# First attention of a gated cross-attention kernel: score products of two steps issued in alternating row halves, and the exponential of odd steps taken straight from PSUM with a bias

## The reference, cut to what matters

```python
xn = _layernorm(x, ln_gamma, ln_beta)
q = (xn @ w_q).reshape(B, SQ, 16, 64)
k, v = split(context @ w_kv)                      # (B, 120, 16, 64) each
scores = einsum('bqhd,bkhd->bhqk', q * 64**-0.5, k)
attn = softmax(scores, axis=-1)
out = einsum('bhqk,bkhd->bqhd', attn, v).reshape(B, SQ, 1024)
out = out @ w_out + b_out
return out * tanh(gate)
```

## Time and profile before

| What | us |
|---|---|
| median of three runs | 334.52 |
| the three runs | 334.09, 334.52, 336.31 |
| span of the profiled execution | 334.5 |
| PE busy | 317.7 (95%) |
| DVE busy | 195.4 (58%) |
| ACT busy | 161.1 (48%) |
| POOL busy | 71.7 (21%) |

### The profile page before, as it was taken

One profiled execution on the slowest core, in us unless ns is written; L12 is line 12 of the kernel. 1 busy time (PEld: TensorE's weight loads), 2 busy tenths in 40 slices (PEclk: granted clock), 3 DMA queues, 4 the chain that ended last, 5 costly groups with the idle time before them and its releaser, 6 DMA issues.

```text
span 334.5 us, 6100 instructions
## 1 busy us (share of the span) xinstructions
PE 317.7 (95%) x2241; PEld 273.2 (82%) x2241; DVE 195.4 (58%) x586; ACT 161.1 (48%) x278; POOL 71.7 (21%) x92
## 2 busy tenths in 40 slices
PE   1999999999999998899996999999999999999995
PEld 1578877888888887798984997889999888998994
DVE  3779768977998986246868483942434162112112
ACT  2483447765664445323353647627533553534530
POOL 1174015667734332010045410100010000000000
PEclk9999999999999999899999999999999999999999
DMA  7799000000000000430000000000000001000001
GB/s 211 233 307 185 0 0 2 3 4 11 19 0 2 0 2 3 145 139 1 0 2 1 2 0 2 0 0 2 3 1 2 0 0 33 0 2 2 0 0 34
DMA packets 10013, 11.31 MB, mean 34 GB/s; under 512 B 1049, under 2 KB 6833, under 8 KB 9984
## 3 DMA queue, kind: packets, MB, share of 16 engines
q1 hardware_dynamic: 9600, 10.55, 10.4%
q0 software_dynamic: 384, 0.36, 1.0%
HBM read 10.39 MB, written 0.52 MB: 33 GB/s over the span
## 4 chain that ended last, share of the span: by engine, by line
PE 82%; DVE 11%; issue 2%; POOL 2%; DMA 2%; ACT 0%; SPq 0%; DVEq 0%
PE bank L1024 28%; PE bank L875 9%; PE bank L876 9%; PE bank L877 8%; PE bank L822 8%; PE bank L831 4%; PE bank L860 4%; DVE xhat_sb L654 3%; PE bank L846 3%; DMA ctx_tok_sb<-in_ctx 2%; PE bank L910 2%; DVE sum_sb L593 2%; DVE negmax_sb L585 1%; PE bank L943 1%; PE bank L957 1%
## 5 line engine op out<-in xcount | busy, mean ns | idle before, releaser
L557 ACT ACTIVATE hT_sb<-bank,cols_sb 128x512 f32<-128x512 f32 x104 | 69.9, 687 | 82.7 <-PE bank L877 81.9
L799 DVE SCALAR_TENSOR_TENSOR x_sb<-bank,wts_sb,x_sb 128x128 f32<-128x128 f32 x128 | 36.0, 344 | 84.2 <-PE bank L1024 84.2
L1024 PEld LDWEIGHTS bank<-we_sb,hT_sb 128*128 128x128 f32 x576 | 66.5, 192 | 1.1
L1024 PE MATMUL bank<-we_sb,hT_sb 128*128 128x128 f32 x576 | 67.2, 275 | 0.0
L462 POOL TENSOR_TENSOR p_sb<-p_sb,recip_sb 128x480 f32<-128x480 f32 x32 | 31.6, 986 | 58.1 <-DVE recip_sb L596 58.1
L822 PE MATMUL bank<-kT_sb,qT_sb 64*128 64x120 f32 x256 | 36.8, 284 | 0.0
L822 PEld LDWEIGHTS bank<-kT_sb,qT_sb 64*128 64x128 f32 x256 | 30.8, 187 | 5.8 <-issue 5.2
L1024 PEld LDWEIGHTS bank<-w_sb,hT_sb 128*128 128x128 f32 x256 | 31.8, 198 | 1.6 <-issue 0.9
L1024 PE MATMUL bank<-w_sb,hT_sb 128*128 128x128 f32 x256 | 32.5, 282 | 0.0
L875 PE MATMUL bank<-xnT_lo_sb,we_hi_sb 128*128 128x512 f32 x72 | 30.4, 422 | 0.0
L876 PE MATMUL bank<-xnT_hi_sb,we_hi_sb 128*128 128x512 f32 x72 | 28.5, 396 | 0.0
(11 more groups left out here) (159 smaller groups left out, 476.0 us busy)
## 6 DMA issues: line engine op xcount, KB each, us to landing
we_sb<-in_L_ffn_We SPq DMA_DIRECT2D x1, 2048.0 KB, 8.3
w_kv_sb<-in_L_xattn_w_kv SPq DMA_DIRECT2D x2, 512.0 KB, 6.6
...
```

Source lines behind the costliest of these rows:

```text
L557: nc.scalar.activation(hT[:, u % 2, c, :], ps(item)[:, :], ACT.Relu if n == 1 else ACT.Silu, bias=cols[:, col:col + 1]).then_inc(read(item ...
L799: last = nc.vector.scalar_tensor_tensor(out=x[:, b, :], in0=ps(item)[:, C * i:C * (i + 1)], scalar=w, in1=x[:, b, :], op0=ALU.mult, op1=AL ...
L1024: last = nc.tensor.matmul(dst[:, C * i:C * (i + 1)], hT[:, slot, c, 128 * i:128 * (i + 1)], wb[:, e, c, :], start=(c == 0), stop=(c == chu ...
```

## The change

1. On TensorE S(i) and S(i+1) are issued together at the even item i, into two banks, and product by product the lower row half (step i) and the upper (step i+1) alternate. At odd items there is no S.
2. S uses four banks (0, 1, 5, 7) in place of two; O is left with bank 4 alone, and other fills with bank 6, which Y has too (`q0` with 4 and 6).
3. The late queries stand as four and four chunks behind items 0 and 1, where they were three, two and three behind items 0, 1 and 2.
4. In odd steps DVE no longer subtracts. It scales the maximum by -1/8 (a `tensor_scalar` on 128x4, L600 of the new kernel), and ACT takes four exponentials of 128x120, one for each head, from PSUM with that number as the bias (L532 of the new kernel). They stand where the one exponential stood, behind the copies of T and O.

```diff
--- before.py
+++ after.py
@@ -91,7 +91,7 @@
 
     schedule += [("q0", c, 0) for c in range(CH)]
 
-    late_queries = ((0, 1, 2), (3, 4), (5, 6, 7))
+    late_queries = ((0, 1, 2, 3), (4, 5, 6, 7))
     for i, chunks in enumerate(late_queries):
         schedule.append(("attend", i))
         schedule += [("q0", c, 1) for c in chunks]
@@ -152,11 +152,12 @@
 
     FILLS = ("ctxT", "cols", "v0", "k0", "xT", "q0", "logits", "wT", "b2", "k1", "v1", "q1", "s1", "pT1", "o1",
              "r1", "up")
+    S0_BANKS = (0, 1, 5, 7)
     turn = 0
     step = -1
     for item in schedule:
         if item[0] in FILLS and 0 <= step < STEPS + LY - 1:
-            spare = (4, 5, 7) if item[0] == "q0" else (0, 1) if item[0] == "up" else (7,)
+            spare = (4, 6) if item[0] == "q0" else (0, 1) if item[0] == "up" else (6,)
             plan(item, spare[turn % len(spare)])
             turn += 1
         elif item[0] in FILLS:
@@ -166,12 +167,13 @@
             plan(item, 6 + unit_at[item[1:]] % 2)
         elif item[0] == "attend":
             i = step = item[1]
-            if i < STEPS:
-                plan(("s0", i), i % 2)
+            if i < STEPS and i % 2 == 0:
+                plan(("s0", i), S0_BANKS[i % 4])
+                plan(("s0", i + 1), S0_BANKS[i % 4 + 1])
             if 0 <= i - LT < STEPS:
                 plan(("pT0", i - LT), 2 + i % 2)
             if 0 <= i - LPV < STEPS and (i - LPV) % 2:
-                plan(("o0", i - LPV), 4 + (i - LPV) // 2 % 2)
+                plan(("o0", i - LPV), 4)
             if 0 <= i - LY < STEPS and (i - LY) % GROUPS == GROUPS - 1:
                 plan(("y0", (i - LY) // GROUPS), 6)
 
@@ -326,6 +328,7 @@
         ident_ready = sem("ident_ready")
         consts_ready = sem("consts_ready")
         exps0_ready = sem("exps0_ready")
+        bias0_ready = sem("bias0_ready")
         recip_ready = sem("recip_ready")
         tanh_ready = sem("tanh_ready")
         dve_chain = sem("dve_chain")
@@ -517,10 +520,18 @@
                             wait_full(act, ("y0", b - 2))
                         copy_out(("o0", j), oT[:, b % 2, half * CH // 2:(half + 1) * CH // 2, :],
                                  ps(("o0", j))[:, :].rearrange("p (c q) -> p c q", q=128))
-                    if i < STEPS:
+                    if i < STEPS and i % 2 == 0:
                         wait_read(act, ("s0", i))
                         nc.scalar.activation(p0[i % 4], p0[i % 4], ACT.Exp, scale=SCALE0) \
                             .then_inc(exps0_ready, 1)
+                    elif i < STEPS:
+                        act.wait_ge(bias0_ready, i // 2 + 1)
+                        if i >= 4:
+                            wait_full(act, ("pT0", i - 4))
+                        for h in range(HG):
+                            last = nc.scalar.activation(p0[i % 4][:, h, :], ps(("s0", i))[:, SK * h:SK * (h + 1)],
+                                                        ACT.Exp, bias=negmax[:, 1, h:h + 1], scale=SCALE0)
+                        last.then_inc(read(("s0", i)), 1)
                 elif kind == "logits":
                     bs = half_of(item[2])
                     shifted += 1
@@ -582,14 +593,23 @@
                     key = ("s0", i)
                     s = ps(key)[:, 0:HG * SK].rearrange("p (h k) -> p h k", h=HG)
                     wait_full(dve, key)
+                    if i % 2 and i >= 2:
+                        wait_read(dve, ("s0", i - 2))
                     link(nc.vector.tensor_reduce(negmax[:, i % 2, :], s, AX, ALU.max))
-                    if i >= 4:
-                        wait_full(dve, ("pT0", i - 4))
-                    nc.vector.tensor_tensor(p0[i % 4], s, negmax[:, i % 2, :].unsqueeze(2)
-                                            .broadcast_to([128, HG, SK]), ALU.subtract).then_inc(read(key), 1)
+                    if i % 2:
+                        nc.vector.tensor_scalar(negmax[:, 1, :], negmax[:, 1, :], -SCALE0, None, ALU.mult) \
+                            .then_inc(bias0_ready, 1)
+                    else:
+                        if i >= 4:
+                            wait_full(dve, ("pT0", i - 4))
+                        nc.vector.tensor_tensor(p0[i % 4], s, negmax[:, 0, :].unsqueeze(2)
+                                                .broadcast_to([128, HG, SK]), ALU.subtract).then_inc(read(key), 1)
                 j = i - 1
                 if 0 <= j < STEPS:
-                    dve.wait_ge(exps0_ready, j + 1)
+                    if j % 2:
+                        wait_read(dve, ("s0", j))
+                    else:
+                        dve.wait_ge(exps0_ready, j // 2 + 1)
                     link(nc.vector.tensor_reduce(sum0[:, j % 2, :], p0[j % 4], AX, ALU.add))
                     if j >= 2:
                         dve.wait_ge(probs_ready, j - 1)
@@ -809,19 +829,21 @@
         def _(pe):
             def attend(i):
 
-                if i < STEPS:
-                    key = ("s0", i)
+                if i < STEPS and i % 2 == 0:
                     b, g = i // GROUPS, i % GROUPS
-                    dst = open_bank(pe, key)
-                    r0 = DH * (g % 2)
+                    dst = [open_bank(pe, ("s0", i)), open_bank(pe, ("s0", i + 1))]
                     for j in range(HG):
                         c = (g // 2) * HG + j
                         if b % HB == 0:
                             wait_read(pe, ("q0", c, b // HB))
                             wait_read(pe, ("k0", c, b // HB))
-                        last = nc.tensor.matmul(dst[:, SK * j:SK * (j + 1)], qT[r0:r0 + DH, c, 128 * b:128 * (b + 1)],
-                                                kT[r0:r0 + DH, c, SK * b:SK * (b + 1)], start=True, stop=True)
-                    last.then_inc(full(key), 1)
+                        for odd in range(2):
+                            r0 = DH * odd
+                            last = nc.tensor.matmul(dst[odd][:, SK * j:SK * (j + 1)],
+                                                    qT[r0:r0 + DH, c, 128 * b:128 * (b + 1)],
+                                                    kT[r0:r0 + DH, c, SK * b:SK * (b + 1)], start=True, stop=True)
+                            if j == HG - 1:
+                                last.then_inc(full(("s0", i + odd)), 1)
                 m = i - LT
                 if 0 <= m < STEPS:
                     key = ("pT0", m)
```

## The result

The changed kernel took 333.18 us (median of 20 runs, 331.92 to 334.91); the kernel before, in 20 runs beside it, 334.58. The ratio is 0.995, with a 95% interval of 0.993 to 0.997: faster by 1.4 us where 5.0 were forecast. It lies in the range of 326 to 335, but by the bound of 1% it is "no change", to which the prediction gave 0.35. The rest of this document is about the 3.6 us that are missing.

A forecast was written before the change was run, and what follows sets the result against it. PE was taken to pace from S(0) to S(18), then DVE to about 129 us; 0.7 + 2.3 + 2.0 + 0.5 - 0.4 = 5.1 off 334.5 gave 329.4, stated as 329.5, range 327.5 to 331.8 (8 in 10: 326 to 335).

The forecast's parts named there:

- Scores on PE: Score matmuls on PE: alternating row halves overlap fully, so two steps' scores take 1.08 us instead of 2.16.
- rival 1: Score matmuls on PE: row halves don't overlap, 1.96 us a pair, total 333.5 to 335, say 334.3; chance 0.2.
- The second T of a pair: Transposes on PE: one group directly behind another needs no array shape change, so 0.45 us in place of 0.58.
- The start: First attention steps: late queries and exponentials delay S(2) to about 50 us; at S(12) the lead is only 0.7 us.
- rival 3: PE's clock falls because of holes, including 1.7 and 1.4 us at T(1) and T(2): total 337.5; chance 0.07.
- The scaling on DVE: Odd steps on DVE: POOL holds up the 128x4 scaling, 0.4 us to the next start, between 0.1 and 0.57 + 0.1.
- a period: Four attention steps where PE paces: 8.05 us of PE work plus a 0.5 wait, 8.6 against 10.48 before.
- the pair without Y: Two attention steps without a Y product, added to one four-step period between S(12) and S(18): 3.6 us.
- DVE's stretch: Step 18 to about 129 us: DVE paces; waits of 1.2 us go and six odd steps give 0.17 each, 2.0 to 2.2.
- rival 2: Odd steps on DVE: scaling not held up, bank stalls smaller, odd steps 1.55 us, total 326.5; chance 0.15.
- The tail: Behind the attention: transposed router weights share bank 6 with the first expert product and wait for its updates, losing 0.4 us.
- ACT: Odd steps on ACT: four exponentials take at most 1.6 us, hidden except where a copy of T is waited for.

The follow-up runs named there:

- the run with halves in turn: Changed kernel with all score products of the lower row half issued first, then all of the upper, without alternation: 336.03 us, ratio 1.001.
- the fillings: Changed kernel with matmuls that compute nothing of the result put in PE's idle holes, two ahead of T(1) and one ahead of T(2): 333.39 us, ratio 0.994.
- the kernel without the scaling: Changed kernel with queries scaled by -1/8 when copied from PSUM and the minimum used directly as the exponentials' bias: 330.27 us, ratio 0.983.
- SP's run: Changed kernel with the eight small loads that POOL issued between its multiplications issued by SP instead: 334.3 us, ratio 0.994.

## Why the prediction was right and wrong

**Scores on PE: right.** 1.08 for two steps was forecast from O, and 1.08 was measured; rival 1 is out, and the run with halves in turn shows that the order of the products does it. The second T of a pair was put at 0.45 and took 0.53 behind Y and 0.55 behind a wait (75.36 to 75.91).

**The start: right but for the clock.** S(2) at 50.19 (forecast about 50), T(1) at 54.70 (54.4), T(2) at 56.56 (56.3). Then O(1) and S(6) ran at the lower clock: S(6) at 58.95 against 57.8, S(12) at 72.61 against 70.7.

**The clock: the step that failed first.** The fall was in the text only as rival 3, with a whole period at the lower level and 337.5 as its time, at 0.07; the sum had no term for it, though the text itself had reckoned with holes of 1.7 and 1.4 us at T(1) and T(2). It came at the two holes that the rival named (T(1) and T(2)), but for some 3 us only. Its size is read from kernels that differ in the fillings alone: the maximum of step 31 at 121.51 without and 119.92 with them, 1.6 us, and this in the execution compared, not in a rare one. The second part is the tail. Of the kernel before, 10 of 23, 14 of 27 and 13 of 18 executions in three sets on one chip ran at the full clock; of the changed kernel none of 20 did, and 19 lost more than one fall's 0.005. (For the 20 executions of before that were timed beside those, the clocks aren't on record; 13 of them took 334.8 us or less, the longest time that went with a full clock elsewhere.) In the span from T(31) to the end both profiled executions have one fall and so the same length (204.2 and 204.25), which hides this in the pair of traces; in the medians of the times it doesn't cancel. The trace of before had shown one dip, in an execution 2 us above the usual one, and the prediction took that as the standing state: it subtracted its 5.1 from the span of an execution with a dip and compared the result with times, where the usual execution of before has none.

The Trainium skill, TensorE: Matmul & The Clock Gate, says under HAM oscillation that idle gaps between bursts bring the clock down. Rows of the changed kernel agree (0.72 behind holes of 1.69 and 1.24), and the fitted fillings remove it there (1.00 in 55 to 60 us). But the kernel before kept 1.00 from 175 to 185 us, around a hole of 2.86 ahead of 179.59, where the changed kernel fell to 0.67 behind the same hole, and the kernel without the scaling kept it behind 1.70 and 0.71; so the gaps allow a fall rather than force it.

**The scaling on DVE: the term that was mis-sized.** The term was 0.4 with 0.57 + 0.1 as the upper bound. Measured were 0.50 behind a multiplication alone (to the next start 0.42), 0.17 with POOL idle, and 1.04 and 1.11 where POOL multiplies, issues a transfer and subtracts. The bound had counted a second operation of POOL's but not the transfer between them, which is part of what POOL does in steps 8 to 15, and which SP's run shows to be half of the cost. So the waits at T at 75.36 and 84.66 were 1.00 and 1.07 instead of 0.5, and a period 9.24 instead of 8.6. (A wait of 1.16 at 66.12 and one of 1.19 at 94.08 stand behind scalings of 0.50 and 0.17: the transfer doesn't explain those.) From S(12) to S(18) that is 0.64 for the period and 0.78 for the pair without Y (4.38 in place of 3.6), 1.4 us together: what is left of the deficit of 3.0 at step 18 when the clock's 1.6 is taken off. That the two add up so exactly is in part chance: at S(12) another 0.3 was missing beside the clock, and the 0.3 by which DVE was to start later behind S(18) didn't come (1.19 against 1.12 before).

**DVE's stretch: right in sum, by two errors that cancel.** From step 18 to step 31 the lead was to grow by 2.0; it grew by 2.35. The forecast held up each scaling by POOL, 0.4 to the next start. Of the seven scalings there five took 0.17 and weren't held (0.07 to the next start at 100.88), which is what rival 2 said, and gave some 0.3 each more than the forecast; and one new wait of 1.22 took most of that back. That one wasn't forecast: the logits' product now fills bank 6, which Y has just used, so PE can start it only when DVE has updated x, and DVE stands until it is done:

```profile
119.42 0.32 DVE L622 SCALAR_TENSOR_TENSOR x_sb<-bank,gA_sb,x_sb 128x128 f32<-128x128 f32 x1
119.79 1.06 PE L965 MATMUL bank<-gate_w_sb,xnT_sb 128*128 128x8 f32 x8 [0.53 <-DVE x_sb L622]
120.96 0.19 DVE L716 TENSOR_TENSOR logits_sb<-bank,gate_b_row_sb 128x32 f32<-128x32 f32 x1 [1.22 <-PE bank L965]
...
122.20 0.17 DVE L600 TENSOR_SCALAR negmax_sb<-negmax_sb 128x4 f32<-128x4 f32 x1
```

The prediction looked for the shared bank in the tail only. No run gives the logits another bank, so what it costs in the end is read from this row and not tested.

**The tail: right.** From T(31) to the transposed router weights were 6.53 us and are 6.87: 0.34 for the bank, where 0.4 was forecast.

**ACT: right.** Four exponentials take 1.12 us of the timeline where 1.6 was the most; ACT waited for the scaling 2.7 us in total, in five places, and no T or O waited for ACT in the steady part.

The sum at the full clock holds nearly: 332.4 - 5.1 = 327.3 was implied as a span, and 328.8 - 0.8 = 328.0 was measured, from three executions. Most of what was missing in the times is the clock, which the changed kernel loses in every execution, and of which the forecast took none. An estimate of how the 3.6 us divide: the median time of before, 334.58, less the 1.85 between time and span is a span of 332.7, so the usual execution of before is 1.8 shorter than the 334.5 that the sum began with, which is what one fall in the tail costs (331.8 to 333.0 against 333.6 to 334.9 in the groups above). The changed kernel's 333.18 less 1.85 is 331.3, which is 1.9 above the 329.4 of the sum; the start's clock is 1.6 of that. T(31) is 1.1 later than forecast for the other reasons, the scaling above all, of which the tail gives some back in a way that isn't traced.
